# First attention layer of a four-layer kernel: normalised probabilities are turned instead of turned inverse sums

## The reference

```python
w_heads = Wqkv @ z + Winj @ u               # per batch, for q, k and v; the two column halves have weights of their own
rq = q + r_w_bias[None, :, :, None]
score = jnp.einsum('bndi,bndj->bnij', rq, k) * SCALE
prob = jax.nn.softmax(score, axis=-1)
attn_vec = jnp.einsum('bnij,bndj->bndi', prob, v)
attn_out = jnp.einsum('od,bdl->bol', Wo, attn_vec) + bo[None, :, None]
x = attn_out + z1ss                          # then a normalisation over the 256 rows
```

## Time and profile before

| | |
|---|---|
| time, median of 3 runs | 3530.7 us (3528.73 to 3533.14) |
| profiled execution, span from first to last instruction | 3531.3 us |
| TensorE busy | 3298.1 us, 93% |
| VectorE busy | 2377.8 us, 67% |
| ScalarE busy | 1780.9 us, 50% |
| GpSimd busy | 202.5 us, 6% |
| mean granted TensorE clock | 0.962 of full speed |
| first layer | about 0 to 1396 us of the span |

### The profile page before, as it was taken

The page is one execution under the profiler, slowest core; times in us unless marked ns, Lnnn a source line. Parts: engine busy times, 40 slices in busy tenths (PEclk is TensorE's granted clock), DMA queues, the critical chain, the costliest instruction groups (busy, mean ns, idle before and its releaser), DMA issues. The chain is left out here.

```text
span 3531.3 us, 55048 instructions
## 1 busy us (share of the span) xinstructions
PE 3298.1 (93%) x21408; PEld 2528.1 (72%) x21408; DVE 2377.8 (67%) x3781; ACT 1780.9 (50%) x4249; POOL 202.5 (6%) x319
## 2 busy tenths in 40 slices
PE   8999999999999997789999998769999999699998
PEld 6777888787777785556666655457887788488885
DVE  6666666666665665599999999537777878542213
ACT  5554444444454443446565554327777777532222
POOL 0000000000000000000000000001111111000000
PEclk9999999999999999989999999779999999899999
DMA  6322212221122211544454544130011110210004
GB/s 216 127 106 101 108 72 81 96 111 72 72 96 90 79 72 59 162 111 115 110 117 110 120 112 111 38 108 13 25 43 62 46 43 31 93 48 24 24 12 162
DMA packets 95697, 300.42 MB, mean 85 GB/s; under 512 B 20144, under 2 KB 28336, under 8 KB 70992
## 3 DMA queue, kind: packets, MB, share of 16 engines
q1 hardware_dynamic: 64960, 186.60, 18.2%
q0 software_dynamic: 12544, 79.70, 6.4%
q10 hardware_dynamic: 17936, 30.59, 2.4%
HBM read 233.95 MB, written 62.91 MB: 84 GB/s over the span
## 5 line engine op out<-in xcount | busy, mean ns | idle before, releaser
L537 ACT ACTIVATE l_prob<-l_bank,l_nmax 128x512 f32<-128x512 f32 x512 | 344.8, 686 | 276.9 <-DVE l_nmax L679 276.9
L679 DVE TENSOR_REDUCE l_nmax<-l_bank 128x1 f32<-128x512 f32 x512 | 317.3, 681 | 71.4 <-PE l_bank L409 71.3
L375 PE MATMUL l_bank<-l_x_hi,l_w_hi 128*128 128x256 f32 x1024 | 297.6, 291 | 11.3 <-DVE l_x_lo L779 11.3
L702 DVE COPY l_probT<-l_bank 128x512 f32<-128x512 f32 x256 | 173.6, 689 | 175.3 <-PE l_bank L423 174.6
L375 PE MATMUL l_bank<-l_x_hi,l_w_lo 128*128 128x256 f32 x1024 | 290.4, 284 | 0.0
L375 PE MATMUL l_bank<-l_x_lo,l_w_hi 128*128 128x256 f32 x1024 | 290.3, 284 | 0.0
L1744 DVE TENSOR_TENSOR_SCAN l_kv<-l_wx,l_kv 128x2056 f32<-128x2056 f32 x64 | 283.8, 4434 | 3.1 <-DVE l_sxc L1865 1.5
L2318 ACT ACTIVATE l2a_sc<-l2a_sc,l2a_nmax 128x256 f32<-128x256 f32 x512 | 254.8, 508 | 41.1 <-DVE l2a_nmax L2434 41.1
L423 PE MATMUL l_bank<-l_ident,l_prob 128*128 128x128 f32 x2048 | 247.9, 275 | 10.6 <-DVE l_k_lo L695 6.3
L423 PEld LDWEIGHTS l_bank<-l_ident,l_prob 128*128 128x128 f32 x2048 | 225.8, 141 | 24.3 <-DVE l_k_lo L695 16.2
L445 PE MATMUL l_bank<-l_probT,l_v 128*64 128x512 f32 x1024 | 233.8, 598 | 0.0
(11 more groups left out here) (351 smaller groups left out, 8177.3 us busy)
## 6 DMA issues: line engine op xcount, KB each, us to landing
l_vb<-vd SPq DMA_DIRECT2D x64, 1024.0 KB
l_w_hi<-kept_w_hi POOLq DMA_DIRECT2D x24, 1024.0 KB, 8.3
l_w_lo<-kept_w_lo POOLq DMA_DIRECT2D x24, 1024.0 KB, 10.3
l_wv_hi<-kept_wv_hi POOLq DMA_DIRECT2D x12, 1024.0 KB, 5.1
l_wv_lo<-kept_wv_lo POOLq DMA_DIRECT2D x12, 1024.0 KB, 7.1
kept_w_hi<-l_w_hi SPq DMA_DIRECT2D x8, 1024.0 KB, 8.7
kept_w_lo<-l_w_lo SPq DMA_DIRECT2D x8, 1024.0 KB, 11.2
l2a_x<-x SPq DMA_DIRECT2D x16, 512.0 KB, 3.6
```

Source lines behind the costliest of these rows:

```text
L375: mm = pe.matmul(s.ap[:, c * ROWS:(c + 1) * ROWS], a[:, kt, c, g, :], b[:, kt, c * ROWS:(c + 1) * ROWS], start=m == 0, stop=m == 3 * KT - 1)
L537: act.activation(prob[h][:, it, :], s.ap[:, :], ACT.Exp, bias=nmax[:, n % 2, it, h:h + 1], accum_out=rsum[:, n % 2, it, h:h + 1]).then_inc ...
L679: dve.tensor_reduce(nmax[:, n % 2, it, h:h + 1], s.ap[:, :], AX.X, ALU.max, negate=True).then_inc(max_ready, 1)
L702: dve.tensor_copy(probT[0][:, j, :], s.ap[:, :]).then_inc(s.drained, 1)
```

## The change

GpSimd no longer spreads the inverse sums. For each of the four query tiles it waits for that tile's inverse sums and multiplies the tile's probabilities of both heads in place, `prob * rinv` (eight instructions of 128x512 a step). TensorE waits for all eight (`prob_ready`) before it turns the probabilities; `turn_sums`, the label `r`, and the tiles `rows`, `rT` and `oT` are gone. VectorE makes the reciprocals in four pieces, three behind the maxima and one behind the queries. ScalarE copies the weighted values to `oT_hi` (`outputs`) between its exponentials, and VectorE subtracts that from the bank for `oT_lo`. TensorE waits for the drained bank in `project_out`.

```diff
--- before.py
+++ after.py
@@ -180,7 +180,7 @@
         if n + 1 < HALF:
             order += [f"k{n + 1}"] + ([f"v{n + 1}_0", f"v{n + 1}_1"] if where(n + 1)[1] % 2 == 0 else [])
         if 0 <= n < HALF:
-            order += [f"t{n}_{j}{h}" for j in range(IT) for h in H2] + [f"r{n}"]
+            order += [f"t{n}_{j}{h}" for j in range(IT) for h in H2]
             order += {BIAS: ["cb"], CENTRE: ["nc_0", "nc_1"], VAR: ["nv"], SPREAD: ["nr"]}.get(n, [])
     plan = [(label, 4 + i % 4) for i, label in enumerate(order)]
     plan += [(f"s{n}_{it}{h}", 2 * (it % 2) + h) for n in range(HALF) for it in range(IT) for h in H2]
@@ -206,9 +206,6 @@
         prob = [ph.sb(f"prob{h}", [P, IT, COLS]) for h in H2]
         probT = [ph.sb(f"probT{h}", [P, IT, COLS]) for h in H2]
         nmax, rsum, rinv = [ph.sb(name, [P, 2, IT, 2]) for name in ("nmax", "rsum", "rinv")]
-        rows = ph.sb("rows", [P, IT, 2, D])
-        rT = ph.sb("rT", [P, COLS])
-        oT = ph.sb("oT", [P, COLS])
         oT_hi, oT_lo = [ph.sb(f"oT_{part}", [P, COLS], F32R) for part in ("hi", "lo")]
         acc = [ph.sb(f"acc{l}", [P, RT, COLS]) for l in range(LANES)]
         wo_raw = probT[0][:, :, :].rearrange("p j i -> p (j i)").rearrange("p (q n) -> p q n", q=HP)
@@ -223,8 +220,7 @@
         w_stored, wv_stored = [ph.sem(f"w_stored{i}") for i in range(2)], ph.sem("wv_stored")
         w_in, wv_in = [kept.enter_context(nc.semaphore(f"kept_w_in{i}")) for i in range(2)], kept.enter_context(nc.semaphore("kept_wv_in"))
         q_hi_ready, q_split, k_hi_ready = ph.sem("q_hi_ready"), ph.sem("q_split"), ph.sem("k_hi_ready")
-        max_ready, rinv_ready, rows_ready = ph.sem("max_ready"), ph.sem("rinv_ready"), ph.sem("rows_ready")
-        oT_ready = ph.sem("oT_ready")
+        max_ready, rinv_ready, prob_ready = ph.sem("max_ready"), ph.sem("rinv_ready"), ph.sem("prob_ready")
         acc_in = [ph.sem(f"acc_in{l}") for l in range(LANES)]
         acc_done = [ph.sem(f"acc_done{l}") for l in range(LANES)]
         acc_stored = [ph.sem(f"acc_stored{l}") for l in range(LANES)]
@@ -339,10 +335,11 @@
                 pool.wait_ge(made, 5)
                 for n in range(HALF):
                     bp, pair, l = where(n)
-                    pool.wait_ge(rinv_ready, n + 1)
-                    if n:
-                        full(pool, S[f"r{n - 1}"])
-                    pool.tensor_copy(rows[:, :, :, :], rinv[:, n % 2, :, :].unsqueeze(3).to_broadcast([P, IT, 2, D])).then_inc(rows_ready, 1)
+                    for it in range(IT):
+                        pool.wait_ge(rinv_ready, IT * n + it + 1)
+                        for h in H2:
+                            pool.tensor_scalar(prob[h][:, it, :], prob[h][:, it, :], rinv[:, n % 2, it, h:h + 1], None, ALU.mult)\
+                                .then_inc(prob_ready, 1)
                     if n == VAR + 1:
                         pool.wait_ge(nvar_ready, 1)
                         pool.tensor_tensor(nrs[:, :], nrs[:, :], power[:, :], ALU.pow).then_inc(nrs_ready, 1)
@@ -411,10 +408,7 @@
                                     mm.then_inc(s.full, 1)
 
                 def turn_probs(n):
-                    drained(pe, S[f"s{n}_{IT - 2}0"])
-                    drained(pe, S[f"s{n}_{IT - 2}1"])
-                    drained(pe, S[f"s{n}_{IT - 1}0"])
-                    drained(pe, S[f"s{n}_{IT - 1}1"])
+                    pe.wait_ge(prob_ready, 2 * IT * (n + 1))
                     for j in range(IT):
                         for h in H2:
                             s = S[f"t{n}_{j}{h}"]
@@ -422,14 +416,6 @@
                             for it in range(IT):
                                 mm = pe.transpose(s.ap[:, it * P:(it + 1) * P], prob[h][:, it, j * P:(j + 1) * P], ident[:, :])
                             mm.then_inc(s.full, 1)
-
-                def turn_sums(n):
-                    s = S[f"r{n}"]
-                    pe.wait_ge(rows_ready, n + 1)
-                    free(pe, s)
-                    for it in range(IT):
-                        mm = pe.transpose(s.ap[:, it * P:(it + 1) * P], rows[:, it, :, :], ident[:, :])
-                    mm.then_inc(s.full, 1)
 
                 def weigh_values(n):
                     bp, pair, l = where(n)
@@ -447,7 +433,7 @@
 
                 def project_out(n):
                     pair = where(n)[1]
-                    pe.wait_ge(oT_ready, n + 1)
+                    drained(pe, S[f"o{n}"])
                     if n == 0:
                         pe.wait_ge(wo_lo_ready, 1)
                     terms = ((wo_hi, oT_hi), (wo_lo, oT_hi), (wo_hi, oT_lo))
@@ -515,7 +501,6 @@
                         project(n + 1, "k")
                         project_v(n + 1)
                     turn_probs(n)
-                    turn_sums(n)
                     if n == BIAS:
                         bias_rows()
                     if n == CENTRE:
@@ -558,12 +543,12 @@
                         full(act, s)
                         act.activation(probT[1][:, j, :], s.ap[:, :], ACT.Copy).then_inc(s.drained, 1)
 
-                def sums(n):
-                    s = S[f"r{n}"]
+                def outputs(n):
+                    s = S[f"o{n}"]
                     full(act, s)
                     if n:
-                        drained(act, S[f"o{n - 1}"])
-                    act.activation(rT[:, :], s.ap[:, :], ACT.Copy).then_inc(s.drained, 1)
+                        full(act, S[f"w{n - 1}_{RT - 1}"])
+                    act.activation(oT_hi[:, :], s.ap[:, :], ACT.Copy).then_inc(oT_hi_ready, 1)
 
                 def split_x(bp, l):
                     act.wait_ge(xraw_in, 32 * (bp * LANES + l))
@@ -645,6 +630,8 @@
                 for n in range(HALF):
                     bp, pair, l = where(n)
                     exponentials(n, (0, 1))
+                    if n:
+                        outputs(n - 1)
                     exponentials(n, (2, 3))
                     if n == 0:
                         split_wo()
@@ -658,7 +645,6 @@
                         keys(n + 1)
                         values(n + 1)
                     probs(n)
-                    sums(n)
                     if n == BIAS:
                         bias_rows()
                     if n == CENTRE:
@@ -667,6 +653,7 @@
                         moments()
                     if n == NORMED:
                         normed()
+                outputs(HALF - 1)
                 act.wait_ge(xn_ready, RT)
 
             @block.vector
@@ -701,22 +688,16 @@
                         full(dve, s)
                         dve.tensor_copy(probT[0][:, j, :], s.ap[:, :]).then_inc(s.drained, 1)
 
-                def reciprocals(n):
-                    drained(dve, S[f"s{n}_{IT - 1}0"])
-                    drained(dve, S[f"s{n}_{IT - 1}1"])
-                    dve.reciprocal(rinv[:, n % 2, :, :], rsum[:, n % 2, :, :]).then_inc(rinv_ready, 1)
+                def reciprocals(n, its):
+                    for it in its:
+                        for h in H2:
+                            drained(dve, S[f"s{n}_{it}{h}"])
+                        dve.reciprocal(rinv[:, n % 2, it, :], rsum[:, n % 2, it, :]).then_inc(rinv_ready, 1)
 
                 def outputs(n):
                     s = S[f"o{n}"]
-                    full(dve, s)
-                    drained(dve, S[f"r{n}"])
-                    if n:
-                        full(dve, S[f"w{n - 1}_{RT - 1}"])
-                    dve.tensor_tensor(oT_hi[:, :], s.ap[:, :], rT[:, :], ALU.mult).then_inc(oT_hi_ready, 1)
-                    dve.tensor_tensor(oT[:, :], s.ap[:, :], rT[:, :], ALU.mult).then_inc(s.drained, 1)
-                    drained(dve, s)
                     dve.wait_ge(oT_hi_ready, n + 1)
-                    dve.tensor_tensor(oT_lo[:, :], oT[:, :], oT_hi[:, :].bitcast(F32), ALU.subtract).then_inc(oT_ready, 1)
+                    dve.tensor_tensor(oT_lo[:, :], s.ap[:, :], oT_hi[:, :].bitcast(F32), ALU.subtract).then_inc(s.drained, 1)
 
                 def add_up(n):
                     bp, pair, l = where(n)
@@ -791,8 +772,10 @@
                     if n:
                         outputs(n - 1)
                     maxima(n, (2, 3))
+                    reciprocals(n, (0, 1, 2))
                     if n + 1 < HALF:
                         queries(n + 1)
+                    reciprocals(n, (3,))
                     if n:
                         add_up(n - 1)
                     if bp == 0 and l == 0 and pair + 1 < HP:
@@ -801,7 +784,6 @@
                         split_wv(pair // 2 + 1)
                     if pair == HP - 1 and bp + 1 < TURNS:
                         split_x(bp + 1, l)
-                    reciprocals(n)
                     if n + 1 < HALF:
                         keys(n + 1)
                     if n == 0:
```

## The result

The changed kernel took 3908.7 us (median of 4 runs, 3905.86 to 3914.81), beside 3531.9 us for the kernel before (4 runs). The ratio is 1.107, with a 95% interval from 1.106 to 1.109: slower by 377 us. Forecast were 3622 us and a range up to 3740. The profiled execution has a span of 3907.4 us.

A forecast was written before the change was run, and what follows sets the result against it. TensorE's instruction stream was taken to bound the first layer. Steps without V +61, with V -16, last step +5, clock +27, splits +15 gave +92 us: 3531.3 to 3623, 3622 for the median; range 3497 to 3740.

The forecast's parts named there:

- What is p?: POOL's time from one 128x512 multiplication's start to the next: taken as 0.95 us, ends 0.56 and 1.35.
- without V: The 32 first-layer steps that do not project the next pair's V: 18.49 us becomes 20.4, together +61 us.
- clock: TensorE's granted clock falls behind its wait for POOL: 1.7 us a drop, half of 32 steps, +27 us.
- splits: Nine steps without V have a DVE split of x or weights inside POOL's run: 1.7 us each, +15 us.
- last step: First layer's last step projects nothing, so PE waits for POOL until S + 16.9 instead of 10.98: +5 us.
- the term 12.8: Step without V lasts 12.8 + 8p: POOL's start at 9.2, 0.1, and 3.5 us for the 32 transposes.
- rival 4: POOL's multiplication costs as the two-input add does, p = 1.35; steps with V wait too: 3765 us, chance 0.14.
- Removed from PE: Four `turn_sums` transposes per step leave TensorE's path: 0.53 us a step, 33 us in 63 steps.
- Moved between DVE and ACT: ACT copies `oT_hi`, DVE subtracts once: maxima and exponentials come 0.69 us earlier, and nothing waits.
- PE's start at S + 9.2 + 8p + 0.1: PE's first transpose follows all eight POOL multiplications; S is the start of the step's scores; before, S + 13.99.
- Steps with V never wait: Where V is projected, POOL ends at S + 16.9 and PE comes at S + 19.76: no wait, -16 us.
- Rival 1 (p = 0.56): POOL multiplies as fast as it copies and ends before PE comes, so no wait: 3499 us, chance 0.16.

The follow-up runs named there:

- experiment 7: Changed kernel with GpSimd multiplying by TENSOR_TENSOR, the inverse sum broadcast along the row, instead of TENSOR_SCALAR: 3678.5 us, ratio 1.042 to the kernel before.
- experiment 1: Changed kernel with GpSimd's multiplications left out, TensorE waiting for the exponentials: 3501.6 us, ratio 0.993 to the kernel before.
- experiments 8 and 9: Changed kernel with earlier reciprocals: 8 gives ScalarE three of the eight tiles, 3508.3 us; 9 keeps all on GpSimd, by TENSOR_TENSOR, 3507.0 us.
- experiment 5: Changed kernel with the first two reciprocals moved ahead of the outputs, so GpSimd starts earlier, all eight multiplications kept: 3596.9 us, ratio 1.019 to the kernel before.
- experiment 2: Changed kernel with GpSimd copying each probability tile onto itself instead of multiplying, all waits kept: 3512.6 us, ratio 0.996 to the kernel before.

## Why the prediction was wrong

**The step that failed is "What is p?".** It put p at 0.95 with an upper end of 1.35; the timeline shows 1.54. It took the row of 552 ns for 128 elements as the starting point and then added the further 384 elements at rates of *other* operations, the copy's 0.69 and the add's 2.2 ns. The row itself, less the 0.26 us that go with any COPY, says 2.3 ns an element, and that line ends at 1.43 us for 512: above the upper end, though still short of the 1.56 that one took. I held the two-input add for an upper bound of a one-input multiplication. It is none: at its 2.2 ns an element 512 would take 1.39 us, and experiment 7 shows a two-input multiplication at 1042 ns where the one-input form takes 1564. Why the one-input form is the dearer one, no run shows.

With p = 1.54 the same working gives: without V 12.8 + 12.3 = 25.1, +6.6 x 32 = +212; with V 25.1 too, +1.3 x 31 = +41; clock, 2.6 x 32 = +83 (325.7 - 64 x 3.71 = 88 by the page); splits +20 (1.57 x 16, less the 0.57 that nine of them lost before); last step +10: +366, and +377 was measured. Another 9 are in the term 12.8: the scores start 3.65 us behind the first transpose (818.76 - 815.11) and not 3.5. With p alone put right, and the clock at +54 and the splits at +15 as rival 4 has them, the sum is +332 instead of +92; so p is most of the miss. The rest is the prices of the clock and of the splits, both too low, and those 9 us.

Point by point:

- *Removed from PE, 33 us.* Right in kind, a little too much: 0.44 us a step, 28 us (experiment 1). The kernels of experiments 8 and 9 have it back, less what the last step costs.
- *Moved between DVE and ACT.* Right. `oT_lo` starts at S + 5.92 (824.68), where before the three operations lasted until S + 7.2; the maxima start 0.7 us earlier and POOL at S + 9.2.
- *PE's start at S + 9.2 + 8p + 0.1.* Right at three values of p, 0.56 (no wait), 1.00 (a wait of 3.1 us) and 1.54 (7.4 us), and with half the work (1.3 us).
- *Steps with V never wait.* Wrong by the same p: 9.2 + 12.3 + 0.1 = 21.6 against PE's 19.8.
- *The clock.* I priced a fall at 1.7 us in half of the steps, from a wait of 2 to 3 us. At 1.9 us (experiment 5) it is just that, 10 of 22, 1.7 us each. At 7.4 us it fell in all 23, and the transposes took about 2.4 us more each.
- *Splits.* I gave nine steps 1.7 us more. The rows say 1.57 us in 13 of the 16 steps with a split, in those with V too, and 1.9 to 3.3 us in the other three. One of the 13, on POOL:

```profile
289.11 13.92 POOL L341 TENSOR_SCALAR l_prob<-l_prob,l_rinv 128x512 f32<-128x512 f32 x8 [14.53 <-DVE l_rinv L695]
```

The split in the middle of it, on DVE, and two of the eight multiplications by themselves:

```profile
293.15 2.29 DVE L728 TENSOR_TENSOR l_wv_lo<-l_wvraw,l_wv_hi 128x2048 fp32r<-128x2048 f32 x1
...
292.19 1.57 POOL L341 TENSOR_SCALAR l_prob<-l_prob,l_rinv 128x512 f32<-128x512 f32 x1
...
293.74 3.13 POOL L341 TENSOR_SCALAR l_prob<-l_prob,l_rinv 128x512 f32<-128x512 f32 x1
```

  Eight multiplications take 13.92 us there instead of 12.35, and the split keeps its 2.29 us. It is POOL that gives way: the multiplication that starts inside the split takes 3.13 us and ends 1.43 us after the split does (296.87 against 295.44), so it lost about what was left of the split when it started, 1.70 us. The rule of the Trainium skill ("SBUF — State Buffer", Who interferes with whom) that a DVE operation with two SBUF inputs and a POOL operation exclude each other is in agreement for this multiplication. For the one ahead of it the trace does not show it: it ran beside the first 0.6 us of the split, and neither was longer for it.
- *Rival 1 (p = 0.56)* did not happen, but experiment 2, at that p, shows that its time, 3499, would have been near: 3512.6. *Rival 4* named the right mechanism, waits in both kinds of step and the clock in every step without V, and was still 144 us short for want of p.
- The Trainium skill ("GPSIMD Engine Reference", 3.1 Elementwise) pointed the other way: its best case of 1.8 cycles an element is 1.5 ns at 1.2 GHz. The rows here say 2.51 ns for TENSOR_SCALAR. The TENSOR_TENSOR with a broadcast operand, a two-input form for which the page gives 2.6 cycles, which is 2.2 ns, came to (1042 - 280) / 512 = 1.49 ns, if the same fixed part is taken for it.

## What to carry to other kernels

When a price must be extended from a single row of the same operation, divide that row first: take off a fixed part that the engine's other rows show, and let its own rate per element be inside the range, however odd it looks beside other operations. Work moved to an idle engine costs nothing up to the moment at which it ends behind the critical engine's other work, and then its full excess in every step; so its start (here two reciprocals, 312 us) and its form (here TENSOR_TENSOR for TENSOR_SCALAR, 3908.7 - 3678.5 = 230 us) matter more than whether it is moved. A wait that has come onto TensorE's path costs its length and the lowered clock behind it, a quarter more here.

## What the runs showed of the hardware that was not expected

- POOL, 128x512 float32: COPY 615 ns, TENSOR_TENSOR with the second operand broadcast from one column 1042 ns, TENSOR_SCALAR with a constant 1491 ns, with a column of multipliers 1564 ns. The form with fewer input elements is the slower one; why was not found.
- TensorE's granted clock behind a wait in a stream that is otherwise dense. Share of waits behind which the 32 transposes took over 5 us instead of 3.7 (which is the lower level, 1.2 GHz, for part of them): 0 of 23 at 1.3 us, 0 of 23 at 1.7 us, 10 of 22 at 1.9 us, 18 of 23 at 3.1 us, 23 of 23 at 3.7 us and at 7.4 us (steps with a split are not counted here). Transposes of a constant tile in the wait kept it at the upper level.
- Of a DVE operation with two SBUF inputs and a POOL operation beside it, the one that started later was stretched, as far as these traces show. In the changed kernel that was the multiplication, which started 0.58 us behind the split; in the later layer it was the DVE operation, which started 0.18 us behind the add and took 2.58 us. Experiment 7 has both. There a multiplication (from 283.64) starts 0.06 us ahead of the split, and the split takes 3.13 us instead of 2.29; the next one starts inside the split and takes 3.09 us instead of 1.04:

```profile
283.64 1.04 POOL L341 TENSOR_TENSOR l_prob<-l_prob,l_rinv 128x512 f32<-128x512 f32 x1
...
283.70 3.13 DVE L723 TENSOR_TENSOR l_w_lo<-l_wraw,l_w_hi 128x2048 fp32r<-128x2048 f32 x1
...
284.64 3.09 POOL L341 TENSOR_TENSOR l_prob<-l_prob,l_rinv 128x512 f32<-128x512 f32 x1
```

  A multiplication of the changed kernel that had run for 0.96 us did not delay the split, so the later one does not always pay. No run changed the order alone.
